# A linear-attention block with a gated mixture of experts: set-up work moved into the first groups, one coefficient transposition in place of four, all scaling on VectorE, and a new order on every engine

## The chip, the cores and the metric

The kernel runs on one core of a Trainium2 chip. Its time is the device time of one execution in microseconds (us); the median over a few executions counts. A profiled execution is a further one, with a time of its own.

## The reference, cut to what matters

The input `x` holds 8 images of 128 channels by 48 x 48 = 2304 tokens. One block is computed:

```python
x = x + conv(ln_c(x))                 # linear attention over tokens, 8 heads of 16
t = to_tokens(x)
t = t + ffn(ln_t(t))                  # 8 experts, the two best per token

# conv: q, k, v = W (x - mean) * rstd + b;  Q = elu(q) + 1;  K = elu(k) + 1
#   den[h] = 1 / (Q[h] . cumsum_over_heads(K)[h] + 1e-10)
#   num[t] = Q[t] . sum over s <= t of K[s] V[s]^T        (causal state, per head)
#   out = num * den
# ffn: logits = t_n @ gate_w + mean(ins @ rmod_w);  p = softmax(logits);  the two largest p are kept
#   out[t] = sum over e of p[t,e] * (gam[e] * (t_n[t] @ expert_w[e] + expert_b[e]) + bet[e])
#   gam = mean(ins @ gamma_w.T);  bet = einsum(ins, beta_w) / 16
```

The expert term is linear in the normalised token, so the kernel folds `gam` into the expert matrices once, folds `gam * expert_b + bet` into one bias row for each expert, and scales the token by `p * rstd` before the matrix product.

## The kernel before, in words

**Tiling.** A chunk is 128 tokens; there are 18 chunks. A group is one chunk of four images (U = 4), so 36 groups run in order, the two halves of the batch alternating (`par`). Channels lie on the 128 partitions of `x`, tokens on the partitions of `qkv`, `feat` and the router's tiles.

**Steps.** Each engine has a program of its own: a function `step(at)` that names, in an order written out by hand, which piece of work of which group comes next. `at(a)` is the group that entered the pipeline `a` steps earlier. `steps` unrolls the first ten steps and the last six (the edge, where `g.edge` adds waits), and runs the rest in a loop of two steps. One step treats one group's worth of work on each engine, so the time from a group to the next (a period) is the same on all engines. Semaphores alone tie the engines together: `need(engine, name, count)` makes an engine wait, and everything behind it on that engine waits too.

**One group.** TensorE (PE) transposes `x` (L911) for the statistics of VectorE (DVE, L612, L620); GpSimd (POOL) makes 1/deviation (L316); ScalarE (ACT) and POOL split `x` into a high and a low part (L421, L307); PE projects (L943 to L945, three products for each image); DVE scales the result into `qkv` (L630), ACT takes exponentials (L427), DVE makes `feat` (L637). POOL sums keys over heads (`cumulative_keys`, L323, L326), multiplies by queries (L332), DVE reduces to the denominators (L643, L649, L654), POOL normalises queries (L338). PE transposes keys (L960) and queries (L975), makes scores (L1000), DVE masks them (`causal`, L659); PE makes key-value products (L1015), the part from the state (L1031) and the values (L1048), all into the bank pair `num`; DVE adds the residual (`attention`, L678), which makes `x1`. PE multiplies `x1` by the centring matrix and the gate (`x1_centred`, L1071), ACT takes squares and logits (L465, L473), POOL the deviation (L361), and DVE ranks the experts in 19 small instructions (`product` to `scales`, L689 to L768).

**The expert part, which the change touches most.** The tile `weight` holds 16 coefficients per token: for each expert p and p * rstd. ACT writes a rounded copy and POOL the remainder, each four times side by side (`coef4`, L486, L366), so that one group has four 128 x 128 blocks. PE transposes the four blocks (L1086) into `bank_g`; ACT copies the result, 512 columns wide, to `coef_t` (L493). Every 32-row band of `coef_t` then holds the same 32 coefficient rows. `spread_scales` (L1128) takes the bands r = 0..3 and spreads expert 4k + r over all partitions, into the four `wide` banks, once for k = 0 and once for k = 1. Then `x1` is multiplied by the spread coefficients for two experts at a time (`xs`): DVE does pairs 0, 1 and 2 from the banks (L774); for pair 3 ACT copies two banks to `spread` (L498) and POOL multiplies (L374). PE multiplies by the experts (L1134, four MATMUL instructions for each pair) on top of the bias (L1093), and DVE adds `x1` (`residual`, L782).

**Set-up.** Before the steps, PE and DVE run `first_weights` (L866: the three projection matrices transposed, centred and split) and `rest_of_weights` (L875: the gate, gammas, router bias, beta, eight expert matrices, the bias rows; DVE's half is L270). The first transposition of `x` comes after both. POOL makes masks and constants, `v_pad` and `state` among them.

## Time and profile before

| what | value |
|---|---|
| median of 3 runs | 734.46 us (734.03 to 735.39) |
| profiled execution, its own time | 737.64 us |
| its span (first to last instruction) | 735.9 us |
| PE busy | 681.8 us (93% of the span), 13757 MATMUL |
| DVE busy | 632.3 us (86%) |
| POOL busy | 468.7 us (64%) |
| ACT busy | 292.0 us (40%) |
| mean granted TensorE clock | 0.978 of full speed |

Busy times of one engine are unions: overlapping instructions count once. An instruction's own time includes its latency, and the next one on that engine often begins before it ends; what an instruction costs its engine is therefore read as the distance from its start to the next start (its pitch). The last 1.7 us of the execution's own time lie outside the span.

### The profile page before, as it was taken

Reading aid. Unit: us, or ns where it says so; the run is one execution under the profiler, and the core shown is the slowest. Engines: PE = TensorE matmul, PEld = TensorE weight load, DVE = VectorE, ACT = ScalarE, POOL = GpSimd, SP = SyncE. Lnnn points to the kernel's source line nnn. Section 1 sums busy time; section 2 is a strip of 40 time slices with the busy share of each in tenths; the row PEclk is TensorE's granted clock in tenths of the full one; section 3 lists DMA queues with packets and bytes.
Section 4 is the critical chain, followed back from the end, with each engine's and each line's share of the span. In section 5 each row is a group of like instructions: output and inputs, shape, how many; then the busy total and the mean of one; then the engine's idle time right before and its main releaser. Section 6 shows DMA issues by size and latency. Waiting matters only on the chain.

```text
span 735.9 us, 35372 instructions
## 1 busy us (share of the span) xinstructions
PE 681.8 (93%) x13757; PEld 458.9 (62%) x13865; DVE 632.3 (86%) x1690; ACT 292.0 (40%) x865; POOL 468.7 (64%) x696
## 2 busy tenths in 40 slices
PE   3667999989999999999999999999999999999986
PEld 1656656656666666666666666666666666665542
DVE  3667999988999999999999999999999999988762
ACT  1134434433444444444444444444444444434311
POOL 5365765565667676767676767676767676764521
PEclk9788999999999999999999999999999999999997
DMA  4111111111111111111111111111111111011000
GB/s 109 53 35 32 45 32 46 46 45 32 45 43 43 43 43 43 43 43 43 43 43 42 44 42 43 42 44 42 44 42 43 42 43 41 29 31 33 17 17 29
DMA packets 60229, 30.53 MB, mean 41 GB/s; under 512 B 2160, under 2 KB 60176, under 8 KB 60176
## 3 DMA queue, kind: packets, MB, share of 16 engines
q1 hardware_dynamic: 60176, 29.79, 14.2%
q8 instruction: 38, 0.62, 0.4%
q14 instruction: 15, 0.12, 0.1%
HBM read 20.34 MB, written 9.44 MB: 40 GB/s over the span
## 4 chain that ended last, share of the span: by engine, by line
PE 82%; issue 8%; POOL 4%; DVE 4%; DMA 1%; ACT 1%; SPq 0%; DVEq 0%; POOLq 0%; ACTq 0%
PE bank_o L1134 31%; PE num L1048 7%; PE num L1031 5%; PE wide_a L1128 4%; PE wide_a L1000 3%; PE num L1015 3%; PE bank_g L1071 3%; PE bank_g L960 3%; PE bank_g L911 3%; PE bank_g L1086 2%; PE bank_g L975 2%; PE wide_a L943 2%; PE bank_o L1093 2%; PE wide_a L945 2%; PE wide_b L943 2%
## 5 line engine op out<-in xcount | busy, mean ns | idle before, releaser
L1134 PE MATMUL bank_o<-xs,e_w 128*128 128x512 f32 x576 | 279.7, 610 | 0.2 <-DVE xs L774 0.2
L1134 PEld LDWEIGHTS bank_o<-xs,e_w 128*128 128x128 f32 x576 | 99.3, 191 | 88.0 <-issue 87.5
L338 POOL TENSOR_TENSOR qn<-feat,rden 128x512 f32<-128x512 f32 x36 | 38.8, 1077 | 114.0 <-DVE rden L654 114.0
L374 POOL TENSOR_TENSOR xs<-spread,x 128x1024 f32<-128x1024 f32 x36 | 97.7, 2714 | 4.4 <-ACT spread L498 4.4
L774 DVE TENSOR_TENSOR xs<-wide_a,x 128x1024 f32<-128x1024 f32 x72 | 87.5, 1215 | 6.2 <-PE wide_b L1128 6.1
L456 ACT ACTIVATE q_eo<-bank_g,parity 128x512 f32<-128x512 f32 x72 | 45.5, 683 | 96.3 <-PE bank_g L975 96.3
L465 ACT ACTIVATE squares<-bank_g 128x128 f32<-128x128 f32 x108 | 28.5, 274 | 137.3 <-issue 70.0
L326 POOL TENSOR_TENSOR k_sum<-k_sum,feat 128x64 f32<-128x64 f32 x216 | 68.8, 318 | 16.9
L637 DVE SCALAR_TENSOR_TENSOR feat<-ex,qkv 128x512 f32<-128x512 f32 x72 | 79.3, 1103 | 0.0
L366 POOL TENSOR_TENSOR coef<-weight,coef 128x256 fp32r<-128x256 f32 x36 | 26.1, 724 | 83.0 <-ACT coef L486 83.0
L307 POOL TENSOR_TENSOR x_low<-x,x_high 128x512 fp32r<-128x512 f32 x36 | 61.1, 1697 | 4.6 <-ACT x_high L421 4.6
L1048 PE MATMUL num<-probs,v_pad 64*32 64x64 f32 x4608 | 55.1, 225 | 8.4 <-issue 7.2
L1048 PEld LDWEIGHTS num<-probs,v_pad 64*32 64x32 f32 x4608 | 48.2, 105 | 8.0 <-issue 7.5
L498 ACT ACTIVATE spread<-wide_b 128x1024 f32<-128x1024 f32 x36 | 36.9, 1025 | 39.3 <-PE wide_b L1128 39.3
L678 DVE TENSOR_TENSOR x<-num,x_res 128x512 f32<-128x512 f32 x36 | 24.9, 692 | 31.2 <-PE num L1048 15.7
L630 DVE SCALAR_TENSOR_TENSOR qkv<-wide_a,rstd,b_qkv 128x384 f32<-128x384 f32 x72 | 43.9, 610 | 4.8 <-PE wide_a L945 2.5
L493 ACT ACTIVATE coef_t<-bank_g 128x512 fp32r<-128x512 f32 x36 | 21.5, 597 | 63.0 <-PE bank_g L1086 63.0
L332 POOL TENSOR_TENSOR qk<-k_sum,feat 128x512 f32<-128x512 f32 x36 | 45.8, 1272 | 0.1
L427 ACT ACTIVATE ex<-qkv 128x512 f32<-128x512 f32 x72 | 45.0, 626 | 1.1 <-issue 1.1
L630 DVE SCALAR_TENSOR_TENSOR qkv<-wide_b,rstd,b_qkv 128x384 f32<-128x384 f32 x72 | 43.9, 610 | 0.7 <-PE wide_b L945 0.7
L1000 PE MATMUL wide_a<-q_eo,k_t 32*64 32x128 f32 x1152 | 42.2, 277 | 2.0 <-issue 1.5
L659 DVE TENSOR_TENSOR probs<-wide_a,tri 128x1024 f32<-128x1024 f32 x36 | 43.5, 1209 | 0.3 <-PE wide_b L1000 0.2
(161 smaller groups left out, 1630.7 us busy)
## 6 DMA issues: line engine op xcount, KB each, us to landing
x<-in_x SPq DMA_DIRECT2D x36, 256.0 KB, 2.9
x_res<-in_x SPq DMA_DIRECT2D x36, 256.0 KB, 2.9
out<-o SPq DMA_DIRECT2D x36, 256.0 KB, 2.5
beta_raw<-in_L_ffn_beta_w SPq DMA_DIRECT2D x1, 512.0 KB
e_raw<-in_L_ffn_expert_w SPq DMA_DIRECT2D x1, 512.0 KB
w_raw<-in_L_conv_Wkv SPq DMA_DIRECT2D x2, 64.0 KB, 2.4
b_qkv<-in_L_conv_bkv SPq DMA_DIRECT2D x1, 128.0 KB, 6.1
w_raw<-in_L_conv_Wq SPq DMA_DIRECT2D x1, 64.0 KB, 2.5
```

Source lines behind the costliest of these rows:

```text
L307: tt(x_low[:, g.par], x[:, g.par], x_high[:, g.par].bitcast(F32), ALU.subtract)\
L326: tt(k_sum[:, :, h], k_sum[:, :, h - 1], f[:, :, 1, h], ALU.add).then_inc(S["cumsum"], 1)
L332: tt(qk[:], k_sum[:].rearrange("p u h d -> p u (h d)"), feat[:, g.par, :, 0:128], ALU.mult)\
L374: tt(xs[:, g.par, 2 * pair:2 * pair + 2], spread[:], flat(x1[:, g.par]).unsqueeze(1) .broadcast_to([128, 2, U * T]), ALU.mult).then_inc(S[ ...
L427: nc.scalar.activation(ex[:, 2 * h:2 * h + 2], qkv[:, g.par, 2 * h:2 * h + 2, 0:256], ACT.Exp, bias=-1.0).then_inc(S[f"ex{h}"], 1)
L456: nc.scalar.activation(q_eo[:, g.par, :, e], bank_g[:].rearrange("p (u t) -> p u t", t=T), copy, scale=parity[:, e:e + 1]).then_inc(S[done ...
L630: stt(qkv[:, g.par, u], w_bank[u][:, 0:384], rstd1[:, g.par, u:u + 1], b_qkv[:], ALU.mult, ALU.add).then_inc(S[f"qkv{u}"], 1)
L637: stt(feat[:, g.par, 2 * h:2 * h + 2], ex[:, 2 * h:2 * h + 2], 1.0, qkv[:, g.par, 2 * h:2 * h + 2, 0:256], ALU.min, ALU.max).then_inc(S[f" ...
L774: tt(xs[:, g.par, 2 * pair:2 * pair + 2], (wide_a, wide_b)[pair % 2][:].rearrange("p (n t) -> p n t", n=2), flat(x1[:, g.par]).unsqueeze(1 ...
L1000: last = mm(w_bank[h][at, T * u:T * u + T], k_t[rows, g.par, u, at], q_eo[rows, g.par, u, :, at], start=True, stop=True, skip_group_check= ...
L1048: last = mm(num[PAIR * h:PAIR * h + PAIR, first:first + SUB], v_pad[at, g.par, u, 2 * h + e], probs[at, g.par, h, u, e], start=False, stop ...
L1134: last = mm(bank_o[:], e_w[:, e], xs[:, g.par, e], start=False, stop=(final and e % 2 == 1), skip_group_check=True)
```

## The change

- **Set-up.** Only `first_weights` stays as one piece, behind the transposition of `x` of the first group. What was `rest_of_weights` is cut into `gammas_and_gate`, `router`, `expert_weights(0)`, `expert_weights(1)`, `expert_bias` and `bias_rows`, which run inside the steps of the first group, all through `bank_o`. DVE takes over from POOL the clearing of `v_pad` and `state`, `place` (copies of the identity) and the selection rows (sums over the identity).
- **Coefficients.** `pack` holds the high and low part once for each image, 32 columns for each of four images, so one 128 x 128 block. PE transposes it once. ACT then writes the four row bands of `coef_t` with 16 copies of 32 partitions x 128 columns.
- **Scaling.** Pair 3 is done by DVE like the others; ACT's `spread_pair`, POOL's `scale_pair` and the tile `spread` are gone.
- **Order.** All five engines have a new order of pieces in a step, with their waits. PE takes the expert pairs as 1, 0, 3, 2 (before: 2, 1, 0, 3), and spreads k = 0 before k = 1. The residual's load is issued a step later, the store two steps later in SP's program.

```diff
 def coef_low_part(g):                                    # POOL
     need(pool, "coef_high", g.i + 1)
     need(pool, "ct_done", g.i)
-    tt(coef4[:, :, :, 1], weight[:].rearrange("p u s e -> p u (s e)").unsqueeze(2)
-       .broadcast_to([128, U, 4, 2 * EXPERTS]), coef4[:, :, :, 0].bitcast(F32), ALU.subtract)\
+    tt(pack[:, :, 1], weight[:].rearrange("p u s e -> p u (s e)"), pack[:, :, 0].bitcast(F32), ALU.subtract)\
         .then_inc(S["coef_low"], 1)
-def scale_pair(g, pair, evac, done):                     # POOL
...
 def coefs(g):                                            # ACT
     need(act, "ct_done", g.i + 1)
     need(act, "spread1", g.i - 1)
-    need(act, "bias_done", g.i - 1)
-    nc.scalar.activation(coef_t[:, g.par], bank_g[:], copy).then_inc(S["ct_evac"], 1)
-def spread_pair(g, bank, scaled, done):
...
+    for r in range(4):
+        for u in range(U):
+            last = nc.scalar.activation(coef_t[ROWS * r:ROWS * r + ROWS, g.par, T * u:T * u + T],
+                                        bank_g[ROWS * u:ROWS * u + ROWS, 0:T], copy)
+    last.then_inc(S["ct_evac"], 1)
...
 def coef_transposed(g):                                  # PE
...
-    for u in range(U):
-        last = transpose(bank_g[:, T * u:T * u + T],
-                         coef4[:, u].rearrange("p r s e -> p (r s e)").bitcast(F32), ident[:])
-    last.then_inc(S["ct_done"], 1)
+    transpose(bank_g[:, 0:T], pack[:].rearrange("p u s e -> p (u s e)").bitcast(F32), ident[:])\
+        .then_inc(S["ct_done"], 1)
...
 def key_values(g):                                       # PE
     need(pe, "feat0", g.i + 1)
     need(pe, "feat1", g.i + 1)
-    need(pe, "kv_masked", g.i)
+    need(pe, "x1_done", g.i)
...
+def gammas_and_gate():                                   # PE; DVE has a function of each name, with the copies
+    pe.wait_ge(S["consts"], CONSTS)
     pe.wait_ge(S["rest_loaded"], 16 * REST_WEIGHTS)
+    transpose(bank_o[:, 0:8], gamma_raw[:], ident[0:EXPERTS, 0:EXPERTS])
+    mm(bank_o[:, 8:16], centre[:], gate_raw[:], start=True, stop=True)
+    mm(bank_o[:, 128:256], ins[:], mean_ins[:], start=True, stop=True).then_inc(S["rest_pe"], 1)
+def router():
+    pe.wait_ge(S["rest_dve"], GATE)
...
+def expert_weights(half):
+    pe.wait_ge(S["rest_dve"], ROUTER + 4 * half)
+    mm(bank_o[:], centre[:], e_raw[:, 4 * half:4 * half + 4], start=True, stop=True).then_inc(S["rest_pe"], 1)
+def expert_bias():
+    pe.wait_ge(S["rest_dve"], EXPERT_W)
...
+def bias_rows():
+    pe.wait_ge(S["rest_dve"], BIASES)
```

The new orders in full, with the age of the group in brackets and the pieces of the first group's set-up left out:

```
PE   experts pair 0 (6); project 2, 3, 1, 0 (2); q_transposed (4); experts 3 (6); scores (4); experts 2, final (6);
     coef_transposed (5); from_state, values (4); spread_scales k=0 (5); k_transposed, key_values (3); bias (5);
     x1_centred (4); experts 1, spread_scales k=1 (5); x_transposed (0), in the first step then first_weights
DVE  ranks_of_others ... scales (5); causal 0, 1 (4); residual (6); features 0, 1 (2); attention (4); scale 1 (5);
     denominators, denominators_eps (3); scale 0 (5); key_values, inverse_denominators (3); scale 3 (5);
     statistics (0); scale 2 (5); product (4); project 2 (1); logits, maximum (4); variances (0); under (4);
     project 1 (1); ranks (4); project 0 (1); first_rank (4); project 3 (1); largest ... equal_to_it (4)
ACT  x_high (0); coefs (5); keys (3); v_odd (2); raw_logits, sum_squares (4); masked_queries (3); router_exp (4);
     first_keys (2); exponentials 0 (1); queries (3); v_even (2); exponentials 1 (1); coef_high (4)
POOL deviation2, coef_low (4); x_low (0); cumulative_keys, query_keys (2); next_state (3); deviation1 (0);
     normalised_queries, middle_state (2)
SP   load x (0); load residual (4); store (8)
```

## Rows read from the trace of the kernel before

**Rows 1.** Timeline of PE: the bias product, once for each group.

```profile
73.32 0.50 PE L1093 MATMUL bank_o<-coef_t,eb_rows 128*128 128x512 f32 x1
...
213.00 0.49 PE L1093 MATMUL bank_o<-coef_t,eb_rows 128*128 128x512 f32 x1
...
635.39 0.51 PE L1093 MATMUL bank_o<-coef_t,eb_rows 128*128 128x512 f32 x1
...
690.38 0.50 PE L1093 MATMUL bank_o<-coef_t,eb_rows 128*128 128x512 f32 x1
```

**Rows 2.** Windows: PE, PEld, DVE, ACT, POOL busy, clock, DMA; one settled period.

```profile
396.60:415.00 18.40, 18.26 (x390) 12.28 (x384) 17.12 (x46) 8.09 (x25) 12.87 (x18) 1.00 0.15 43
```

**Rows 3.** Chain that ended last, settled periods: start, time, what.

```profile
388.06 0.76 PE num L1015 x48
...
392.58 0.44 PE bank_g L1086 x4
...
394.15 0.43 PE wide_a L1128
...
394.59 0.59 PE bank_g L960 x4
...
395.21 1.48 PE num L1048 x91
396.69 0.42 PE bank_o L1093
...
399.47 0.70 PE bank_g L1071 x6
...
400.39 1.72 PE bank_o L1134 x4
```

**Rows 4.** Timeline of DVE, one settled period: start, own time, what.

```profile
401.08 1.32 DVE L637 SCALAR_TENSOR_TENSOR feat<-ex,qkv 128x512 f32<-128x512 f32 x1
...
402.74 0.62 DVE L630 SCALAR_TENSOR_TENSOR qkv<-wide_a,rstd,b_qkv 128x384 f32<-128x384 f32 x1
...
404.93 0.21 DVE L689 TENSOR_TENSOR lg<-lg_raw,rstd 128x32 f32<-128x32 f32 x1
...
409.10 0.19 DVE L768 TENSOR_TENSOR weight<-weight,rstd 128x32 f32<-128x32 f32 x1
409.20 0.89 DVE L612 BATCH_NORM_STATS2 bn<-bank_g 128x6 f32<-128x128 f32 x4
410.01 1.21 DVE L659 TENSOR_TENSOR probs<-wide_a,tri 128x1024 f32<-128x1024 f32 x1
...
412.26 0.68 DVE L782 TENSOR_TENSOR o<-bank_o,x 128x512 f32<-128x512 f32 x1
...
417.17 0.68 DVE L637 SCALAR_TENSOR_TENSOR feat<-ex,qkv 128x512 f32<-128x512 f32 x1
417.76 1.22 DVE L774 TENSOR_TENSOR xs<-wide_a,x 128x1024 f32<-128x1024 f32 x1
```

**Rows 5.** Timeline of POOL: pair 3 in a settled and in an early period.

```profile
399.03 2.81 POOL L374 TENSOR_TENSOR xs<-spread,x 128x1024 f32<-128x1024 f32 x1
...
115.26 2.35 POOL L374 TENSOR_TENSOR xs<-spread,x 128x1024 f32<-128x1024 f32 x1
```

**Rows 6.** Timeline of DVE, the same early period.

```profile
115.29 2.86 DVE L637 SCALAR_TENSOR_TENSOR feat<-ex,qkv 128x512 f32<-128x512 f32 x1
```

**Rows 7.** Timeline of ACT: a copy-like instruction of 128 columns, and the next.

```profile
400.48 0.28 ACT L465 ACTIVATE squares<-bank_g 128x128 f32<-128x128 f32 x1 [3.51 <-issue]
400.65 0.19 ACT L465 ACTIVATION_READ_ACCUMULATOR squares<-bank_g 128x1 f32 x1
```

**Rows 8.** Timeline of the start: PE, PE and DVE.

```profile
13.94 0.27 PE L878 MATMUL num<-ident,gamma_raw 8*128 8x8 f32 x1 [1.24 <-DVE w_low L570]
...
26.19 1.12 PE L911 MATMUL bank_g<-ident,x 128*128 128x128 f32 x4 [1.03 <-DVE eb_rows L604]
...
30.87 0.59 DVE L630 SCALAR_TENSOR_TENSOR qkv<-wide_a,rstd,b_qkv 128x384 f32<-128x384 f32 x1
```

More of the change, by code:

```diff
@@ L177, in need, with first @@
                 eng.wait_ge(S[name], count)
+        def first(g):
+            return g.edge and g.i == 0
         def flat(v):
@@ new lines, in first_weights @@
+                for k in range(2):
+                    for part in range(2):
+                        at = 4 * k + 2 * EXPERTS * part
+                        nc.vector.reduce_sum(sel_parts[:, k, part:part + 1], ident[:, at:at + 3 * ROWS + 4:ROWS + 1],
+                                             axis=AX).then_inc(done, 1)
+                dve.wait_ge(done, 19)
+                nc.vector.reduce_sum(sel_rows[:], sel_parts[:], axis=AX).then_inc(done, 1)
+                dve.wait_ge(done, 20)
+                copy(sel[:], sel_rows[:].unsqueeze(2).broadcast_to([128, 2, 128])).then_inc(done, 1)
@@ L826, in step @@
                     scales(g)
-                g = at(0)
-                if g:
-                    statistics(g)
+                    if first(g):
+                        bias_rows()
                 g = at(4)
@@ L839, in step @@
                     denominators(g)
+                    denominators_eps(g)
+                g = at(5)
+                if g:
+                    scale_pair(g, 0, "spread0", "scaled0")
+                g = at(3)
+                if g:
+                    key_values(g)
+                    inverse_denominators(g)
+                    if first(g):
+                        router()
+                g = at(5)
+                if g:
+                    scale_pair(g, 3, "spread1", "scaled3")
+                g = at(0)
+                if g:
+                    statistics(g)
                 g = at(5)
```

543 lines of the change are left out of this document (268 added, 275 removed).

## Prediction

> **What bounds the kernel now.** I read the shares of the page first, then the pace of the groups, then one settled period on each engine, then start and end.
>
> The bias product runs once in each group, so its starts are the pulse of the kernel [rows 1]. Groups 0 to 7 take 139.7 us (19.95 each), groups 7 to 30 take 422.4 us (23 periods of 18.365), groups 30 to 33 another 55.0, and 45.5 us follow until the span ends at 735.9. With the 73.3 ahead of the first, that is the whole span: 73.3 + 139.7 + 422.4 + 55.0 + 45.5 = 735.9. The early groups cost 139.7 - 7 x 18.365 = 11.1 us more than settled ones.
>
> In a settled period PE is busy 18.26 of 18.40 us at a granted clock of 1.00, DVE 17.12 [rows 2]. The chain that ended last lies on PE there [rows 3]. So PE is the bound, but DVE is only about a microsecond behind, and any work given to it must be counted.
>
> The early groups show another limit. While POOL multiplies pair 3 from 115.26 on, DVE's `feat`, begun 0.03 us later, takes 2.86 us [rows 5, 6]; undisturbed it takes 0.68 [rows 4]. It ends about when POOL's 2.35 us and one `feat` after another would. In a settled period the same meets the other half of `feat`: started at 401.08 with POOL's product running from 399.03 to 401.84, it takes 1.32, 0.64 too long [rows 4, 5]. Both read two operands from SBUF. I take it that the two engines shut each other out for whole instructions.
>
> **The change, part by part.**
>
> *One transposition in place of four.* Four take 0.44 us on PE [rows 3], 0.11 each. Three go: -0.33. PE's own period becomes 18.365 - 0.33 = 18.03. That is the floor.
>
> *Pair 3 on DVE.* An instruction of this shape is priced by the two `causal` ones, 410.01 to 412.26: 1.13 each [rows 4]. DVE goes from 17.12 to 18.25. Against it: `feat` no longer meets POOL's product, -0.64 settled (it can still meet POOL's key sums and x_low; bounds 0 to -0.64, I take all but a few tenths). And the 19 router instructions, 404.93 to 409.20, cost 0.225 each, because each waits for the one before; one whose successor is independent costs 0.10 (409.10 to 409.20) [rows 4]. The new order puts other work behind product, maximum, under, ranks and first_rank: 5 x 0.125 = -0.6. `denominators_eps` loses such cover, +0.1. DVE needs about 17.2, under PE's floor.
>
> *The loop through both engines.* Busy sums are not enough, since PE and DVE now hand work to each other twice in each period. DVE does pairs 3 and 2 only after PE's second spreading; `causal` comes only after pair 3 (1.13), statistics (0.81, 409.20 to 410.01), pair 2 (1.13), four projections (2.19, 402.74 to 404.93), variances (0.34, from the end of `feat` at 402.40 to 402.74), the router (4.27 - 0.6 = 3.67); with `causal` itself (2.25) that makes 11.52 [rows 4]. Then PE's values may start, and until the second spreading PE has values 1.48, spreading 0.43, key transposition 0.59, key-values 0.76, bias 0.42, x1_centred 0.70 x 8/6 = 0.93, experts 1.72, spreading 0.43: 6.76 [rows 3]. One turn: 18.28 us, plus handovers. It is longer than PE's floor, so I put the period at 18.3. `key_values` has a new wait, on `attention`: behind `causal` DVE has residual, two `feat` and `attention` (some 2.4), PE has values, spreading and key transposition (2.50), so it just fits; each tenth that `feat` is held up delays key_values, bias, x1_centred and the experts behind it.
>
> *16 small copies on ACT.* Before, one copy of 512 columns stood between transposition and spreading. A 128-column instruction on ACT lasts 0.28, and the next begins 0.17 later [rows 7]. Bounds for 32 partitions x 128 columns: 0.17 each overlapped, 2.8 us in all; 0.28 each without overlap, 4.5 us. I take 0.17, the pitch that the row shows. The cover on PE is from_state (393.02, where the transpositions end, to 394.15, 1.13) and values 1.48: 2.61 [rows 3]. Exposed: 0.2, which falls into the wait that values has for `causal` anyway; I take 0. If the cover is gone, the excess over about 2.8 us falls on PE in every period, since all four bands must be there.
>
> The Trainium skill ("ScalarE: Activation LUTs", What ACT_TABLE_LOAD costs) gives such an instruction 186 ns + 0.833 ns for each element and an overlap of 93 ns: 0.20 for each copy, 3.3 us in all (an estimate from that page). By that figure up to 0.7 us a period would be exposed and the time would be about 733 to 739; the row's pitch is shorter, and no run here shows a copy of 32 partitions.
>
> *ACT, POOL.* ACT has 8.09 busy of 18.40 and POOL 12.87 [rows 2]; ACT gains some 2, POOL loses over 2.8. ACT's and POOL's removed multiplications, the narrower coefficient parts and SP's later residual and store cost nothing on the path: PE and DVE cover them, and SP's loads, residuals and stores now wait for groups that were done a period before. If a residual came late, `attention` would stand, and key_values behind it.
>
> *The early groups.* The 2.86 us `feat` goes with POOL's product [rows 5, 6], so I let the early periods be 18.3 too: -11.1.
>
> *The start.* What came between 13.94 and the first transposition of x at 26.19, 12.25 us, leaves the start; from there to the first scaled projection at 30.87 are 4.68 [rows 8]. With x transposed ahead of the weights, I expect that projection at about 17, as statistics and deviation still follow DVE's set-up: -14. DVE's added set-up (some 12 short ones) and POOL's shorter one I let cancel. The removed 12.25 us come back inside the first groups as six handovers between PE and DVE: bounds 0 (hidden in PE's gaps of the fill) and 12.25 (all in line); I take 7. Net -7, so the first bias product at 66.3 (59 to 72).
>
> *The end.* In the last groups nothing covers ACT's copies (2.8 for 0.6 before, three groups) or the DVE pair; POOL's 2.4 to 2.8 goes. Bounds -3 to +6; I take +2: 47.5.
>
> *Sum.* 66.3 + 33 x 18.3 + 47.5 = 717.7 of span. The profiled execution's own 737.64 is 1.74 over its span, and the median is 3.18 under that execution: the median lies 1.4 under the span. So **716 us**, 18 less than 734.46. Of the 18, 11 come from the early groups, 7 from the start, some 2 from settled periods; 2 are lost at the end.
>
> **The rivals.**
>
> *DVE takes PE's place.* For it: 17.12 + 1.13 = 18.25, and in the laid-out order DVE stands about half a microsecond before the second spreading is there; if the router gains nothing and `feat` is held by POOL's key sums as long as before, the period is 18.75. Against it: the 0.64 and the 0.6. 66.3 + 33 x 18.75 + 47.5 - 1.4 = 731.
>
> The Trainium skill ("Perfetto Trace Analysis", Optimizing Scalar/DVE Operations) advises handing work away from a saturated DVE; the change hands it work, and by that rule this rival is the likelier one. It adds that POOL and DVE share a read port, so that moving work between them might not help, which is what the 2.86 us row bears out.
>
> *ACT's copies set the pace* (the rival on the other side). One mechanism: 16 copies without enough overlap, between transposition and first spreading. Without overlap 4.5 us, 1.7 to 1.9 beyond the cover: period 20.1, 66.3 + 33 x 20.1 + 47.5 - 1.4 = 776. It decides from 0.56 us of excess on (18.5 / 33), which is 0.2 for each copy. Against it: the 0.17 pitch, and that they depend on nothing among themselves.
>
> *The change does not do what it says.* The 12.25 us are all in line again, the early groups stay at 19.95 (another POOL read holds `feat`), settled ones at 18.365: 71.6 + 139.7 + 477.4 + 47.5 - 1.4 = 735.
>
> **How the numbers follow.** Forecast (705 to 726): 0.60. DVE as bound (726 to 735): 0.15. ACT's copies (over 737): 0.15. No gain: 0.05. Better than all this, at PE's floor with a hidden set-up (594 + 59 + 46 - 1.4 = 698): 0.05. Two tenths of a per cent, 1.5 us, is what a measurement can tell here. Faster: 0.60 + 0.05 + most of 0.15 = 0.80; slower: the copies, 0.15; same: 0.05. The range leaves out the far part of the copies and the lowest case: 702 to 739; the forecast's own is 705 to 726.
>
> **What would show it.** Right: settled bias products 18.2 to 18.4 apart, the first seven no slower, first bias near 66, `feat` near 0.7 (under 1.2), ACT's copies 0.17 apart and their last before PE needs them. Wrong: PE standing before the first spreading with ACT as releaser (copies); PE standing before values or key_values with DVE as releaser and DVE without gaps (DVE bound); first bias after 72 (set-up in line).

## The result, and the profile after

The changed kernel takes 829.09 us (median of 4 runs, 825.03 to 834.26), the kernel before, measured beside it, 734.25: a ratio of 1.130, 95% interval 1.123 to 1.137. It is 13% slower, where I had forecast 2.5% faster. The profiled execution spans 823.0 us, against 735.9.

The bias product is the pulse again; it is line L1118 now, and these are its starts in groups 0, 7 and 33 on PE's timeline, to be held against [rows 1].

```profile
70.80 0.47 PE L1118 MATMUL bank_o<-coef_t,eb_rows 128*128 128x512 f32 x1
...
224.80 0.79 PE L1118 MATMUL bank_o<-coef_t,eb_rows 128*128 128x512 f32 x1
...
772.40 0.50 PE L1118 MATMUL bank_o<-coef_t,eb_rows 128*128 128x512 f32 x1
```

| stretch | before, us | forecast | after | after - before |
|---|---|---|---|---|
| ahead of the first bias product | 73.3 | 66.3 | 70.8 | -2.5 |
| groups 0 to 7 (the opening) | 139.7 | 128.1 | 154.0 | +14.3 |
| groups 7 to 33 | 477.4 | 475.8 | 547.6 | +70.2 |
| behind group 33 | 45.5 | 47.5 | 50.6 | +5.1 |

The four differences add up to 87.1, that of the spans. Most of it, 70.2 us, lies in the settled groups: 21.06 us each, where the forecast had 18.3. The page's groups of the changed kernel name the place (behind the bars: busy us and mean ns of one; then the engine's idle us ahead of it, and what ended most of that).

```profile
L468 ACT ACTIVATE coef_t<-bank_g 32x128 fp32r<-32x128 f32 x576 | 154.7, 269 | 19.7 <-PE bank_g L1110 12.9
...
L1153 PE MATMUL wide_a<-coef_t,sel 32*128 32x512 f32 x144 | 38.2, 526 | 59.3 <-ACT coef_t L468 58.8
```

The 576 copies keep ACT busy for 154.7 us, 0.27 each, with no time shared between neighbours, and PE stands 58.8 us ahead of the first spreading until they are done. One period on PE's timeline shows it (start, own time, what; idle ahead of it in brackets):

```profile
450.24 0.27 PE L1110 MATMUL bank_g<-ident,pack 128*128 128x128 f32 x1
...
451.83 1.48 PE L1071 MATMUL num<-probs,v_pad 64*32 64x64 f32 x128 [0.20 <-issue]
455.07 0.49 PE L1153 MATMUL wide_a<-coef_t,sel 32*128 32x512 f32 x2 [1.75 <-ACT coef_t L468]
```

and in another period ACT's timeline has all 16 copies as one line:

```profile
407.42 4.47 ACT L468 ACTIVATE coef_t<-bank_g 32x128 fp32r<-32x128 f32 x16 [0.36 <-PE bank_g L1110]
```

4.47 us for 16 is 0.28 each. After transposition, from_state and values PE has nothing to do for 1.75 us. That is not the whole price. The windows of the stretch behind this stop follow (PE, PEld, DVE, ACT, POOL busy; then the granted clock; DMA):

```profile
453.31:455.07 1.76, 0.01 (x3) 0.01 (x2) 0.95 (x2) 1.63 (x7) 1.52 (x4) 1.00 1.10 324
455.07:456.19 1.12, 1.09 (x8) 0.70 (x10) 0.57 (x1) 0.00 (x0) 1.12 (x2) 0.98 0.31 92
456.19:457.01 0.82, 0.82 (x64) 0.76 (x64) 0.82 (x2) 0.82 (x2) 0.74 (x3) 0.50 0.00 0
457.01:460.00 2.99, 2.99 (x17) 2.65 (x12) 2.49 (x6) 0.43 (x5) 0.88 (x2) 0.57 0.00 0
460.00:462.00 2.00, 2.00 (x10) 0.76 (x9) 0.15 (x1) 0.95 (x8) 1.92 (x4) 1.00 0.00 0
```

PE resumes at full clock, and 1.1 us later, busy all the time, it is granted 0.50 and 0.57 for 3.8 us: the lower level, 1.2 GHz in place of 2.4, for most of that time. By the granted share, this is work of 0.82 x 0.50 + 2.99 x 0.57 = 2.1 us at full clock (an estimate from these windows). In some periods this does not happen, as windows of two whole periods show:

```profile
435.00:457.00 22.00, 19.99 (x385) 13.33 (x381) 16.67 (x47) 10.61 (x39) 9.30 (x17) 0.89 0.12 36
...
523.00:542.90 19.90, 17.89 (x388) 11.84 (x381) 17.09 (x48) 10.62 (x39) 9.80 (x18) 1.00 0.13 40
```

A period without clock loss (three of the 26) takes 19.90, the mean 21.06: some 1.2 us a period are the clock's.

### The profile page after: what moved, and what is told of

It is laid out like the page before. It is cut to its first block, busy times and chain, and to the rows that moved or that the text cites. A ratio compares the mean times of both kernels' runs of the same rounds, so it can differ in the third digit from the quotient of the medians.

```text
span 823.0 us, 35561 instructions
## 1 busy us (share of the span) xinstructions
PE 708.4 (86%) x13649; PEld 468.4 (57%) x13757; DVE 631.1 (77%) x1737; ACT 386.0 (47%) x1369; POOL 359.1 (44%) x637
## 4 chain that ended last, share of the span: by engine, by line
PE 73%; ACT 17%; issue 7%; DVE 2%; POOL 0%; ACTq 0%; POOLq 0%; DVEq 0%
PE bank_o L1159 31%; ACT coef_t L468 17%; PE bank_g L1096 4%; PE wide_a L1153 4%; PE wide_a L1019 4%; PE num L1036 4%; PE bank_g L979 3%; PE bank_g L930 3%; PE bank_o L1118 2%; PE wide_a L962 2%; PE bank_g L994 2%; PE wide_b L1019 2%; PE wide_b L962 2%; PE wide_a L964 2%; PE wide_a L963 2%
## 5 line engine op out<-in xcount | busy, mean ns | idle before, releaser
L761 DVE TENSOR_TENSOR xs<-wide_b,x 128x1024 f32<-128x1024 f32 x72 | 88.2, 1225 | 126.0 <-PE wide_b L1153 126.0
L468 ACT ACTIVATE coef_t<-bank_g 32x128 fp32r<-32x128 f32 x576 | 154.7, 269 | 19.7 <-PE bank_g L1110 12.9
L430 ACT ACTIVATE q_eo<-bank_g,parity 128x512 f32<-128x512 f32 x72 | 45.6, 684 | 213.4 <-PE bank_g L994 213.4
L353 POOL TENSOR_TENSOR pack<-weight,pack 128x64 fp32r<-128x64 f32 x36 | 11.5, 321 | 291.4 <-ACT pack L460 291.4
L311 POOL TENSOR_TENSOR k_sum<-k_sum,feat 128x64 f32<-128x64 f32 x216 | 90.2, 418 | 16.9
L1153 PE MATMUL wide_a<-coef_t,sel 32*128 32x512 f32 x144 | 38.2, 526 | 59.3 <-ACT coef_t L468 58.8
L1153 PEld LDWEIGHTS wide_a<-coef_t,sel 32*128 32x128 f32 x144 | 14.2, 192 | 93.8 <-ACT coef_t L468 64.4
L1019 PEld LDWEIGHTS wide_a<-q_eo,k_t 32*64 32x64 f32 x1152 | 34.9, 134 | 33.5 <-issue 33.5
L625 DVE SCALAR_TENSOR_TENSOR feat<-ex,qkv 128x512 f32<-128x512 f32 x72 | 51.9, 760 | 0.5 <-ACT ex L397 0.3
L418 ACT ACTIVATE k_t<-bank_g 128x512 f32<-128x512 f32 x36 | 21.5, 598 | 57.8 <-PE bank_g L979 57.8
L292 POOL TENSOR_TENSOR x_low<-x,x_high 128x512 fp32r<-128x512 f32 x36 | 45.9, 1274 | 3.9 <-ACT x_high L391 3.9
```

The lines of the kernel that those rows point to most:

```text
L292: tt(x_low[:, g.par], x[:, g.par], x_high[:, g.par].bitcast(F32), ALU.subtract)\
L311: tt(k_sum[:, :, h], k_sum[:, :, h - 1], f[:, :, 1, h], ALU.add).then_inc(S["cumsum"], 1)
L430: nc.scalar.activation(q_eo[:, g.par, :, e], bank_g[:].rearrange("p (u t) -> p u t", t=T), copy, scale=parity[:, e:e + 1]).then_inc(S[done ...
L468: last = nc.scalar.activation(coef_t[ROWS * r:ROWS * r + ROWS, g.par, T * u:T * u + T], bank_g[ROWS * u:ROWS * u + ROWS, 0:T], copy)
L625: stt(feat[:, g.par, 2 * h:2 * h + 2], ex[:, 2 * h:2 * h + 2], 1.0, qkv[:, g.par, 2 * h:2 * h + 2, 0:256], ALU.min, ALU.max).then_inc(S[f" ...
L761: tt(xs[:, g.par, 2 * pair:2 * pair + 2], (wide_a, wide_b)[pair % 2][:].rearrange("p (n t) -> p n t", n=2), flat(x1[:, g.par]).unsqueeze(1 ...
```

## The experiments

A run for which no ratio is given is a single execution. The kernel before took 728.8 to 739.1 us in its executions, so a few microseconds between single runs say little. A period is the mean of groups 7 to 30, if no other stretch is named.

### Are the copies the cause, and what of them?

**Old coefficients in the new order** (e1). `coef4`, four transpositions and one 512-column copy, all else as changed:

```diff
-  transpose(bank_g[:, 0:T], pack[all four images])
+  for u in range(U): transpose(bank_g[:, T*u:T*u+T], coef4[:, u])
-  for r in range(4): for u in range(U): copy(coef_t[band r, T*u:T*u+T], bank_g[band u, 0:T])
+  copy(coef_t[:], bank_g[:])          # and the coefficients four times side by side
```

> The changed kernel with the coefficient part undone: four-fold coef4, four transpositions, one copy of 512 columns on ACT; the new order, the set-up in parts and pair 3 on DVE stay. Theory A (the 16 copies, 4.5 us a period, hold PE up by 1.9 us, and the standing PE costs 1.4 us more through its granted clock): settled period 18.2 to 18.7, clock 1.00 in settled windows, 705 to 735 us. Rival B (the new order and pair 3 on DVE cost most of it): period stays above 20, 780 us or more.

784.81 us (ratio 1.069, 1.062 to 1.076). The clock is 1.00 in settled groups and the period 19.34. So the copies cost 44 us over the path that they replaced, but the new order with the old path is slow by itself: theory A's 705 to 735 is refuted, and there is more than one cause. One part of it is the old path's own: GpSimd's low part is four times as wide again, and PE waits for it ahead of the transposition, 0.55 us each time (PE's waits from 300 to 600 us: total, times, longest):

```profile
PE bank_g L1109 <- POOL coef L353: 8.3, 15, 0.9
```

**PE kept busy** (e2). Two 128x512 products without use ahead of the first spreading, so PE works where it stood:

```diff
+  ...                               # not in the first group; bank_o must be free
+  for _ in range(2): mm(bank_o[:], centre[:], e_w[:, 0:4], start=True, stop=True)
   spread_scales(g, 0, "spread0")
```

> The changed kernel with two more matrix products of 128 x 512 (1.7 us at full clock, result not used) on PE in every group but the first, put into the gap ahead of the first spreading. Theory A, second half (the gap costs clock): granted clock back at 0.98 or more in settled windows, period 19.9 to 20.2, 775 to 790 us, faster with more work. Rival C (the clock has another cause, or does not matter): the clock stays near 0.93 and the period at 21.3 or more, 829 us or above.

802.49 us (ratio 1.095, 1.088 to 1.101), 27 us faster than the changed kernel, with more work on PE. PE's timeline shows the products in the gap (one line, x4):

```profile
415.26 1.49 PE L1071 MATMUL num<-probs,v_pad 64*32 64x64 f32 x128
416.67 1.98 PE L1206 MATMUL bank_o<-e_w,centre 128*128 128x512 f32 x4
418.59 0.50 PE L1153 MATMUL wide_a<-coef_t,sel 32*128 32x512 f32 x2
```

Now the granted clock is 1.00 from 300 to 600 us and the period 20.2, as theory A said; the time lies above its 775 to 790. The copies are as slow as before, 4.46 us. So the clock's loss comes from PE's stop, and the copies cost beyond it.

**No shift between partitions** (e3): each copy reads the band that it writes, so the spreading reads other coefficients.

```diff
-  copy(coef_t[band r, T*u:T*u+T], bank_g[band u, 0:T])
+  copy(coef_t[band r, T*u:T*u+T], bank_g[band r, 0:T])
```

> The changed kernel, but each of the 16 copies reads the row band that it writes (no move between partitions); the coefficients of three of four images are then other images' ones, so the output is not the reference's. If the move between partitions is what keeps the copies from overlapping: they come 0.17 us apart, 2.8 us in all, and the time falls to 720 to 760. If it is the 32 partitions, or anything else: 0.28 apart still, 4.5 us, time as in the changed kernel.

**All 128 partitions** (e4): 16 copies of 128x128, twelve into a spare tile; again other coefficients.

```diff
-  copy(coef_t[band r, T*u:T*u+T], bank_g[band u, 0:T])
+  copy(coef_t[:, T*u:T*u+T] if r == 3 else spare[:, r, T*u:T*u+T], bank_g[:, 0:T])
```

> The changed kernel, but each of the 16 copies takes all 128 partitions x 128 columns (12 into a spare tile, 4 into coef_t; the coefficients are wrong for three of four images, so the output is not the reference's). If 32 of 128 partitions are what keeps the copies from overlapping: 0.17 us apart, 2.8 us in all, 720 to 760 us. If a row of equal copies out of one bank is what does it: 0.28 apart, time as in the changed kernel.

e3 takes 755.65 us, e4 752.42. ACT's timelines of e3 and then of e4:

```profile
423.27 3.05 ACT L468 ACTIVATE coef_t<-bank_g 32x128 fp32r<-32x128 f32 x16 [0.36 <-PE bank_g L1110]
```

```profile
403.40 2.15 ACT L470 ACTIVATE spare<-bank_g 128x128 fp32r<-128x128 f32 x12
405.30 0.93 ACT L470 ACTIVATE coef_t<-bank_g 128x128 fp32r<-128x128 f32 x4
```

The same number of copies, of four times the partitions, goes by at 0.16 each (1.90 us from the first to the thirteenth), and 32-partition copies at 0.19. The clock is 1.00 in settled groups, the periods 18.71 and 18.62. So 73 to 77 us of the 95 lost hang on the pitch of the copies, and their number is not the reason.

**Band order** (e5) and **source order** (e9) ask what hinders the overlap: e5 reads the band that it writes but takes another at every copy; e9 has the change's own copies, with the four that read one band behind each other.

```diff
 # e5, against the change                    # e9, against the change
-  for r in range(4): for u in range(U):     -  for r in range(4): for u in range(U):
+  for u in range(U): for r in range(4):     +  for u in range(U): for r in range(4):
-    copy(coef_t[band r], bank_g[band u])         copy(coef_t[band r], bank_g[band u])
+    copy(coef_t[band r], bank_g[band r])
```

> The changed kernel, its 16 copies each reading the band of partitions that they write (as in the run without shift), but with another band at every copy, as the changed kernel's have it; the coefficients that the spreading reads are therefore not the right ones. In the changed kernel the copies start 0.28 us apart, without the shift and with one band for four copies in a row 0.185. Theory A, the shift between partitions keeps a copy from starting under the one before: still about 0.185 apart, 16 in some 3.0 us, and 753 to 759 us. Rival B, it is the change of band from one copy to the next: 0.28 apart, 4.5 us, and 820 to 834 us.

> The changed kernel with its 16 copies in another order alone: the four row groups of one tile follow each other, so that four copies in a row read the same band of partitions, and the band that is written changes at every copy. The run in band order (a new band read and written at every copy) kept the 0.28 us of the changed kernel, the run without shift (read and written band change at every fourth copy) had 0.185. Theory A, a copy that reads another band than the one before can't start under it: 0.18 to 0.21 us apart, some 3.1 us for the 16, and 753 to 768 us. Rival B, it is enough that either band changes: 0.28 us, and 820 to 834 us.

e5 takes 834.57 us and its 16 copies 4.46 (0.28 each); e9 takes 852.30, and ACT's timeline has:

```profile
420.45 4.47 ACT L468 ACTIVATE coef_t<-bank_g 32x128 fp32r<-32x128 f32 x16 [0.36 <-PE bank_g L1110]
```

My theory fell twice: it is not the shift (e5 has none), and not the band that is read alone (in e9 it stays for four copies, and in the change's own order the written band does). In all runs a copy begins 0.28 after the last when either band differs from the last one's, and about 0.16 after it otherwise: by that e3, with a change at 3 of 15 steps, would need 3 x 0.28 + 12 x 0.16 and 0.26 for the last copy itself, 3.02 us, and its line says 3.05. That e9 is slower than the change by 23 us with equal copies is the clock: 0.886 in the mean against 0.927; why it falls more often there I have not settled.

**TensorE writes the bands** (e6): 16 products with the identity in place of transposition and small copies, then one 512-column copy. **Four wide copies** (e10): the four images' coefficients are transposed into one and the same band, and copied four times 32x512.

```diff
 # e6
+  for u in range(U): for r in range(4): mm(bank_g[band r, T*u:T*u+T], pack[:, u], ident[:])
+  copy(coef_t[:], bank_g[:])
 # e10
+  for u in range(U): transpose(bank_g[0:32, T*u:T*u+T], pack[:, u])
+  for r in range(4): copy(coef_t[band r], bank_g[0:32])
```

> The changed kernel, with TensorE writing the four row groups itself: 16 products of a tile's 32 coefficients with the identity, one for each row group and tile, each into its band of the bank, and then one ScalarE copy of 128x512 as before the change (0.6 us). The single transposition and the 16 small copies go. Theory A (the small copies and the clock that the gap costs are what the change loses in a settled group): the wait of the first spreading goes, the granted clock is 1.00 in settled groups, a period is 18.4 to 18.9 us as in the two runs with faster copies, and the time is 745 to 760 us; it stays above 734 because the opening still takes some 150 us. Rival B (TensorE's time is what counts, and 16 small products cost more than they save): a period above 19.4 us and a time above 780 us.

> The changed kernel with four transpositions, each of one tile's 32 coefficients into the same 32 partitions of the bank, and four copies of 32x512, one for each row group, in place of one transposition and 16 copies of 32x128. TensorE takes some 0.35 us more in a period. Theory A (the changed kernel loses by the time until the coefficients are there, and by the clock behind that): copies of 32x512 take 0.60 us as one of 128x512 does, and no more than 0.6 apart, so 2.4 us or less in place of 4.5; the first spreading no longer waits, the clock is 1.00 in settled groups, a period is 18.6 to 19.0 us (VectorE's and GpSimd's loop), and the time is 750 to 762 us. Rival B (TensorE's own time is what counts now, as in the run with 16 products): a period over 19.0 us and 770 us or more.

e6: 777.19 us (ratio 1.058, 1.051 to 1.065), period 19.03, clock 1.00, PE busy 296.4 of 300 us: PE's own time took over, so period and time lie between A's and B's. e10: 764.48 us (ratio 1.038, 1.032 to 1.045), period 18.70, and

```profile
404.36 2.38 ACT L467 ACTIVATE coef_t<-bank_g 32x512 fp32r<-32x512 f32 x4 [0.43 <-PE bank_g L1109]
```

2.38 for four, 0.60 each: no overlap either, since the written band changes, but 4 fixed costs in place of 16. PE no longer waits for the copies, as theory A said. It ends 12 us behind e4 although the settled period is only 0.07 longer: from group 30 on it needs 110.3 us to the end, e4 100.4. In these last groups, where the code is written out, PE's stops that the trace puts down to issue add up to 8.1 us from group 30 to 34 in e10 and to 2.2 in e4; what such stops are comes under "The opening".

**The copies in the order before** (e16): only the coefficient path is changed.

```diff
+  pack, one transposition and 16 copies in the kernel before; pair 3 and every order as before
```

> The kernel before with the coefficient path of the change alone: coefficients of one quarter of the width, one transposition, 16 small copies; all orders and pair 3 as before. Between the transposition and the first spreading TensorE has only the 64 products from the state to do (1.1 us). Theory A (the copies' 4.5 us stand open in TensorE's order, less these 1.1 us and the 0.4 us that the transposition saves, and the clock falls behind the gap): TensorE waits 2.7 to 3.3 us in each period, the granted clock is below 1.00, a period is 20.8 to 23.5 us, and the time is 815 to 910 us. Rival B (ScalarE's later work, the copy of pair 3 and the keys behind the coefficients, moves with it and sets a longer period): over 23.5 us, and over 910 us. Rival C (the copies are hidden in this order): a period under 18.6 us.

911.91 us. PE's waits from 300 to 600 us (total, times, longest):

```profile
PE wide_a L1129 <- ACT coef_t L494: 45.6, 13, 3.6
```

In this stretch the period is 23.9 and the clock 0.86. PE is busy 248.9 of 300 us, 19.8 a period at that clock, and waits 3.6 a period for the copies (45.6 us over 12.5 periods): 23.4 of the 23.9. Period and time are B's numbers, but the place is A's, with a larger wait (2.7 to 3.3 expected) and clock loss than I had worked out; ACT's work behind the copies shows in no wait of PE.

### The opening

**Six more groups written out**, ahead of the loop, with the loop's instructions: e8 on e4, e13 on the kernel before.

```diff
-  first = (depth + 4) // PAR
+  first = (depth + 4) // PAR + 3
```

> The run with 16 copies of all 128 partitions (752.42 us; the twelve extra copies go into a spare tile and the spreading reads coefficients that are not the right ones), with six more groups written out ahead of the loop, on every engine, by the same instructions and waits that the loop has. In the opening of all runs of the changed order TensorE stands still 0.5 to 1.7 us at a time inside its runs of 64 to 128 small products, for nothing that the trace names, and a period is 20 to 24 us. Theory A (instructions of straight-line code reach TensorE more slowly than it uses them up in runs of small products): the six groups run at 20 to 23 us like the opening, each has such stops, the granted clock is below 1.00 in them, and the time is 762 to 780 us. Rival B (the opening is long because of what the first groups wait for, weights and a pipeline that is not yet full): the six groups run at 18.3 to 19.0 us and the time stays within 3 us of 752 us.

> The kernel before with six more groups written out ahead of the loop, on every engine, by the same instructions and waits that the loop has. In the changed order the same edit made these six groups some 2.7 us longer each, with stops of TensorE in its runs of small products, and cost 25 us. Theory A (straight-line code costs the order before too; its first groups of 20.0 us are long for this reason): the six groups run at 19.3 to 20.5 us in place of 18.36, and the time is 740 to 750 us. Rival B (only the changed order suffers, since its stops come where the clock falls): the six stay within 0.3 us of 18.36 us, and the time is within 3 us of 734 us.

The six groups run from group 6 to 12. There e8 takes 126.6 us and e4 111.6: 2.5 more each, at a clock of 0.93, with 9.4 us of stops: theory A. It ends at 777.63, 25 us more, partly since the written-out last groups grew too. PE's waits of e8 from 222 to 350 us, then the DMA view's instruction queues in that stretch (packets, MB, share):

```profile
PE num L1037 <- issue: 8.6, 6, 2.3
PE num L1072 <- issue: 0.9, 5, 0.2
```

```profile
q8 instruction: 17, 0.28, 0.8%
q14 instruction: 7, 0.06, 0.1%
```

In e4 neither queue moves a packet in the same stretch: code is fetched where it is written out, not inside the loop. The stops stand in or right behind runs of small products, and no wait is named for them. But the packets' own times fit them. One example, of e4's opening: a packet of 16 KB on q8 goes from 196.10 to 197.12 us, and PE stands still from 197.45 to 198.51:

```profile
198.51 0.88 PE L1072 MATMUL num<-probs,v_pad 64*32 64x64 f32 x68 [1.06 <-issue]
```

In all runs together, PE has 117 stops of over 1 us put down to issue behind the first bias product. Of these, 113 end 2.2 to 3.0 us after a packet on q8 began, though such packets come some 6 us apart; of 57 other stops of that length not more than 12 us behind a packet, 8 do. Together with e8 this says that PE waits for its code in these stops.

The kernel before is different: 737.72 us in e13, groups 6 to 12 in 112.6 against 110.2, 0.4 more each, and stops of 1.2 us in all in these groups. Neither theory's number; nearer to B. That the total is so near 734 is in part chance: e13 has its first bias product 6.0 us earlier than the profile before, with the same set-up, and takes 5.7 us more from group 30 on.

**The code moved on** (e14): 128 idle weight loads ahead of PE's first step, in e4.

```diff
+  pe.wait_ge(S["consts"], CONSTS)
+  for _ in range(128): nc.tensor.ldweights(blank[:], tile_position=(0, 0))
   steps(pe, step, 6)
```

> The run with 16 copies of all 128 partitions (752.42 us; the spreading reads coefficients that are not the right ones), with 128 idle weight loads ahead of TensorE's first step, while it would wait for the first weights anyway, so that all its later instructions lie 128 further on in the code. Theory A (the stops come where the next piece of code has not landed, and fall at other products when the pieces end elsewhere, but are as many): the opening from the first bias to the eighth stays within 4 us of 152.0 us, and its stops move to other products. Rival B (the place where the pieces end decides): the opening changes by more than 6 us, down to 140 us or up to 160 us.

763.83 us. The opening is 153.2 us (A: within 4 of 152.0), with a stop of 2.2 us at the keys' transposition, where e4's longest is 1.4. PE's stops add up to 13.8 us in it, to 13.4 in e4. So where the pieces end moves the stops and does not remove them. From group 30 on it needs 9 us more than e4.

**Shorter runs of small products**: e11 first mends GpSimd's order in e10, e12 puts the products from the state ahead of a long product, e17 takes the keys' and values' products out of the run in e10.

```diff
 # e11 against e10, POOL: ... deviation2, cumulative_keys, coef_low_part, x_low_part, query_keys ...
 # e12 against e11, PE:   ... scores, from_state, experts 2, coef_transposed, values, spread 0 ...
 # e17 against e10, PE:   ... bias, x1_centred, experts 1, spread 1, key_values, x_transposed ...
 #                  DVE:  key_values behind scale_pair 3
```

> The run with four wide copies, with one part of GpSimd's order more: the sums of the keys are made ahead of the low part of the coefficients, not behind it and x's low part. In the runs with fast copies VectorE waits 0.6 us in each period for the product of the key sums, while GpSimd stands still 6.8 us ahead of the coefficients' low part. Theory A (this wait is what keeps the settled period at 18.6 us instead of TensorE's 18.0): the wait goes and a period is 18.0 to 18.4 us, 28 of them give 6 to 15 us back, and the time is 738 to 750 us. Rival B (another wait takes its place at once: TensorE's transposition for the low part of the coefficients, or the sums' meeting with VectorE's work): the period falls by less than 0.15 us, and the time by less than 4 us.

> The run with key sums first, with one part of TensorE's order more: the 64 products from the state stand ahead of the last two experts' product and the transposition of the coefficients, not between that and the 128 products of the values, so that a stretch of four long products lies between the runs of small ones. Theory A (in the opening, which is straight-line code, runs of small products use up instructions faster than they arrive, and a long product between them lets them catch up, as the order before had it): the seven opening groups take 138 to 147 us instead of some 150, the settled periods stay within 0.15 us, and the time falls by 5 to 12 us to 728 to 743 us. Rival B (only the number of instructions counts, wherever they stand): the opening stays within 3 us of the run with key sums first.

> The run with four wide copies (764.48 us), with the 64 products of keys and values moved behind pair 1's products and the second spreading on TensorE, and their masking behind pair 3 on VectorE. In the order before, the row of small products between two long ones is 192 (64 from the state, 128 values); in the changed order it is 256, since keys and values follow; here it is 192 again. Theory A (the length of the row of small products decides how often a piece of code has not landed): the opening falls from 151.5 us to 140 to 147 us, stops at the keys' products go, and with the settled period between 18.4 and 18.75 us the time is 745 to 758 us. Rival B (the stops stay as many, at other products): the opening stays within 3 us of 151.5 us, and the time within 5 us of 764 us, or as far below as the settled period falls.

e11: 770.87 us (ratio 1.049, 1.042 to 1.056), period 18.81. VectorE's waits from 300 to 600 us, first of e10 and then of e11:

```profile
DVE den L629 <- POOL qk L317: 8.7, 16, 0.7
DVE xs L759 <- PE wide_b L1153: 2.8, 9, 0.4
```

```profile
DVE xs L763 <- PE wide_b L1157: 11.9, 16, 0.8
```

The wait for the key sums is gone and one for the second spreading stands in its place: rival B. VectorE works ahead of the spreading and then waits at it. PE in turn waits in each period, ahead of the keys' products, for the `x1` that DVE's `attention` makes:

```profile
PE num L1038 <- DVE x L667: 4.4, 16, 0.4
```

So each engine waits for the other: the joint loop of PE and DVE that I had laid out is the bound, not GpSimd.

e12: 781.80 us (ratio 1.061, 1.055 to 1.068), period 19.34, opening 151.8; e17: 785.05 (ratio 1.067, 1.063 to 1.072), period 19.50, opening 147.5. By the opening, e12 is rival B's case, and e17 lies between the two theories; both times lie above any that was expected. Both lost in the settled period what I wanted to keep: e12 by a wait for the copies, since the transposition now comes later, e17 by x1_centred waiting 0.9 for pair 1. In the opening, PE's stops (those put down to issue) add up to 16.0 us in e10, 15.7 in e11, 10.9 in e12 and 10.4 in e17; in e17 none is left at the keys' products. Of e10 and then of e17, PE's waits from 70 to 222 us:

```profile
PE num L1034 <- issue: 5.5, 4, 2.4
PE wide_a L1153 <- issue: 4.8, 4, 3.8
PE num L1069 <- issue: 3.4, 3, 1.3
```

```profile
PE wide_a L1155 <- issue: 5.0, 4, 4.1
PE bank_g L1096 <- DVE xs L759: 2.8, 3, 1.0
PE num L1071 <- issue: 2.7, 3, 1.4
```

So the length of the runs matters, but it accounts for some 5 of 16 us of stops; in e12 the opening is no shorter for it, and neither time fell.

### Pair 3 on VectorE

**Alone, in the order before** (e7), and with the denominators' sum behind both pairs (e15):

```diff
 # e7: POOL's scale_pair 3 and ACT's spread_pair go; on DVE
    scale_pair(g, 2, "spread1", "scaled2")
+   scale_pair(g, 3, "spread1", "scaled3")
 # e15: DVE's denominators(g) moved from ahead of these two to behind them
```

> The kernel before with one part of the change alone: pair 3 is scaled by VectorE straight out of the bank, right behind pair 2, and ScalarE's copy of it and GpSimd's product (2.4 us) go. Theory A (GpSimd's long product under the second feature instruction is what makes the early groups long, and VectorE has 1.2 us to spare in a settled period of 18.36 us): the seven opening groups fall from 139.7 us to 128 to 133 us, a settled period stays 18.3 to 18.6 us, and the time is 720 to 732 us. Rival B (VectorE has nothing to spare, because its order makes it wait for TensorE): a settled period of 18.9 to 19.6 us, and 745 to 775 us. Rival C (the opening's length comes from TensorE's own unrolled code and not from the feature instruction): the opening stays within 2 us of 139.7 us, the period within 0.1 us, and the time within 3 us of 734 us.

> The run with pair 3 alone on VectorE in the order before (741.87 us, settled period 18.76 us), with the denominators' sum behind pairs 2 and 3 in VectorE's order, not ahead of them, so that both pairs are done 0.6 us earlier. There TensorE waited 0.4 us in each period for pair 3 ahead of the second spreading. Theory A (this wait is the whole of the 0.40 us by which the period grew): the wait goes, the period is 18.30 to 18.45 us, the opening stays near 136 us, and the time is 727 to 733 us, faster than before. Rival B (VectorE's row of work is full, and the next wait comes at once, for x1 or pair 1): a period of 18.6 us or more, and 738 us or more.

e7: 741.87 us (ratio 1.011, 1.007 to 1.015). The first bias product comes 4.0 us earlier, the opening is 136.1 (3.6 less), and the settled period 18.76, 0.39 more: none of the three theories has these numbers. PE's waits from 300 to 600 us, e7 and then e15:

```profile
PE wide_a L1125 <- DVE xs L770: 6.6, 16, 0.4
```

```profile
PE bank_g L1069 <- DVE xs L770: 9.1, 16, 0.6
```

The wait that VectorE's added 1.13 us brings is 0.41 a period. e15: 756.77 us (ratio 1.027, 1.024 to 1.030): the wait ahead of the spreading went, and one ahead of x1_centred of 0.57 came, since attention and pair 1 are later. The period is 19.18, and the opening 140.8: rival B. No version that I ran beats the kernel before.

## Why the prediction was wrong

**The step that failed: "I take 0.17, the pitch that the row shows."** The row [rows 7] is an instruction on all 128 partitions, and what follows it there is the reading of its accumulator on the same partitions, not a second copy. The copies are another thing: each reads or writes another band than the one before, and the pitch of that is 0.28 (the changed kernel, e5, e9), the upper bound that I had written beside it; without such changes it is 0.16 (e4). I reasoned that the copies depend on nothing among themselves. That was so, and did not decide it. The Trainium skill ("ScalarE: Activation LUTs", What ACT_TABLE_LOAD costs) gave an estimate of 0.20, by an overlap of neighbours. The rows of e4 (0.16) and e3 (0.19 in the mean) agree that neighbours overlap; those of the changed kernel, 0.28 apart at 0.27 of own time, do not.

**The cover** was worked out right: 2.61 us of PE's work, 4.5 needed, 1.9 exposed; the trace has 1.75 in the period shown. The rival "ACT's copies set the pace" named mechanism, place and price, with 20.1 a period, and a period at full clock takes 19.90. Its 776 us is short of 829 by what it left out: the lower clock behind each stop (21.06 - 19.90 = 1.16 a period, 30 us in the 26 settled groups, which e2 bears out: when PE did not stop, these groups gave 19 us back although the added products made each some 0.4 longer than 19.90), the opening, where I had 20.1 and 22.0 was measured (13 us), the start (4.5 us) and the end (3 us). Two smaller terms, 19.90 for 20.1 (-5) and a median 6 us above the profiled span where I had 1.4 below (+7), nearly cancel. My chance of 0.15 rested on the wrong pitch.

**"The early groups": -11.1** failed as well: I took one held instruction for the whole of the excess. `feat` did get shorter, 0.76 in the mean, down from 1.10. But no wait of PE in the opening before names it. What PE waited for there was POOL's low part of `x`, which stands right behind pair 3's product in POOL's order (PE's timeline of the kernel before):

```profile
119.39 0.42 PE L943 MATMUL wide_a<-w_high,x_high 128*128 128x384 f32 x1 [0.73 <-POOL x_low L307]
```

These waits and one for a pair come to 3.0 us in the seven groups. With pair 3 alone moved (e7) they are gone, and the opening is 3.6 us shorter. Another 4.7 us were PE's own stops in written-out code (3.3 at L1048), which were in the trace, and I read past them. In the changed order such stops are 13.4 us, at a clock of 0.96, and the waits for ACT's copies add 6.4.

**"The loop through both engines": 18.28.** With fast copies the period is 18.62 to 18.71. The path was the right one, and I left out its handovers. In e4 the two steps of the loop differ: groups take 18.30 and 18.95 us by turns. From `causal` to PE's values are 2.5 us in both (2.25 in my sum), from values to pair 3 7.1 to 7.2 (6.76): 0.6 to 0.7 more than I had. From pair 3 to `causal` DVE needs 9.23 in one step, as I had it (9.27), and 8.69 in the other. Half of that difference is a gap ahead of the first piece of DVE's step, which comes every second time (e4, DVE's timeline):

```profile
437.74 0.19 DVE L721 TENSOR_TENSOR rank<-equal,order 128x32 f32<-128x32 f32 x1 [0.32 <-DVE equal L717]
```

So half of the groups meet the 18.3 with a shorter router and longer handovers, and the mean does not. e11 shows that to take one wait away brings the next one. It costs 6 us in 26 groups against the 18.365 before, and the floor of 18.03 is not reached.

**"DVE takes PE's place"** (731 us) has its nearest measure in e7, in the order before: 18.76 a period, where that rival had 18.75 in the new one; that the two figures agree so closely is chance. The advice of the Trainium skill beside it ("Perfetto Trace Analysis", Optimizing Scalar/DVE Operations), to hand work away from a saturated VectorE, agrees with that row: 0.39 us a period for handing it 1.13.

**The start.** First scaled projection at 16.20 (about 17 forecast); first bias product at 70.8, inside 59 to 72 but not 66.3. From the one to the other it takes 54.6 us, 42.4 before: the 12.25 us came back. Whether they came back as the handovers that I had named is not shown; the clock is 0.75 in this stretch, 0.83 before. Nor is the gain of 2.5 us clear of the spread, as the kernel before with the same set-up has its first bias product at 73.3 in one profile and at 67.4 in another (e13). **The end:** 50.6 for 47.5, inside its bounds; e4, with fast copies, has 45.3.

**What adds up.** From before to e4 the span grows by 14.5 us: -3.5 ahead of the first bias product, +12.3 opening, +6.0 settled, -0.3 end. From e4 to the changed kernel by 72.6: +1.0, +2.0, +64.3, +5.3. The first sum is what the change would have cost with fast copies: it is slower than before even then.

**Open.** Why the order before loses so little to written-out code: e13 fetches as much of it in its six groups as e8 (19 packets on q8, 18 in e8), with 1.2 us of stops for 9.4, and runs as long as its own (e12, e17) still stop for 10 us. And why the stops in the last groups come to 2.2 us in e4 and to 8.1 in e10 and 9.0 in e14, with the same order and close to the same code, which is most of the 10 us by which their ends differ.

## What to carry to other kernels

Take the price of an instruction from a row with the same partitions in the same succession, not only of the same size; where the bounds differ by 0.1 us and it runs 16 times on the path, measure it alone before building on it. A stop of PE is to be priced with the clock behind it, here 1.2 us on top of 1.8. Where two engines hand work to each other twice in a period, moving work to the one that is a microsecond behind costs a wait at once, and mending that wait brings the next (e7, e15; e11 for another wait in such a loop).

## What the runs showed of the hardware

- ScalarE copies from PSUM follow each other by 0.16 us on the same partitions, and by 0.28 (32x128) when the band that is read or the band that is written changes. Copies of 32x512 whose written band changes follow by 0.60, their own time.
- After a stop of 1.76 us PE resumed at full clock and was granted 0.50 and 0.57 from 1.1 us later on, over 3.8 us; with work in the gap (e2) the clock stayed at 1.00 from 300 to 600 us.
- Written-out code costs PE stops of up to 4.1 us (e17) in or right behind runs of small products. An instruction queue moves 17 packets (0.28 MB) in six such groups of e8, and none in e4's loop; 113 of 117 such stops of over 1 us end 2.2 to 3.0 us after a packet on it began.
